# Two-layer attention and mixture-of-experts kernel: the loads of both accumulators wait for both last scatters

## The reference

```
x = x + cross_attention(norm(x), keys and values = ctx and the tokens themselves)   # layer 0
x = x + experts(norm(x), 8 experts, each token goes to 2, inner width 256)          # layer 0
x = x + cross_attention(norm(x), keys = values = ctx, masked)                       # layer 1
x = x + experts(norm(x), 32 experts, each token goes to 8, inner width 192)         # layer 1
experts(t) = sum over the chosen e of weight(t, e) * (silu(t @ gate_e) * (t @ up_e)) @ down_e
```

## Time and profile before

| | us |
|---|---|
| median of three runs | 943.73 |
| lowest and highest of them | 940.0 and 945.9 |
| the profiled execution, its time | 939.34 |
| its span, from the first to the last instruction | 937.6 |

### The profile page before, as it was taken

The page is one execution under the profiler, slowest core; times in us unless marked ns, Lnnn a source line. Parts: engine busy times, 40 slices in busy tenths (PEclk is TensorE's granted clock), DMA queues, the critical chain, the costliest instruction groups (busy, mean ns, idle before and its releaser), DMA issues.

```text
span 937.6 us, 19263 instructions
## 1 busy us (share of the span) xinstructions
PE 796.3 (85%) x5266; PEld 437.7 (47%) x5267; DVE 559.9 (60%) x1596; ACT 516.6 (55%) x780; POOL 433.0 (46%) x355
## 2 busy tenths in 40 slices
PE   4999999999848999966888735999889899999995
PEld 2444455555425544433443414555555455555552
DVE  5553445555564555685676625576557575667475
ACT  6533234455445776333544523786777787778760
POOL 3882000200014676130075662467776666667862
PEclk9999999999968999998899876999999999999998
DMA  8562200201116696790120102898899897998777
GB/s 287 180 217 98 77 34 23 46 24 35 34 26 207 181 253 147 213 315 7 53 69 26 48 24 67 219 261 251 202 253 262 234 303 192 250 223 260 143 112 276
DMA packets 85842, 143.74 MB, mean 153 GB/s; under 512 B 19462, under 2 KB 36102, under 8 KB 85793
## 3 DMA queue, kind: packets, MB, share of 16 engines
q1 hardware_dynamic: 58880, 93.49, 30.5%
q0 software_dynamic: 24320, 49.45, 24.4%
q10 hardware_dynamic: 2592, 0.19, 0.2%
HBM read 106.25 MB, written 41.28 MB: 157 GB/s over the span
## 4 chain that ended last, share of the span: by engine, by line
PE 49%; issue 13%; DMA 12%; DVE 11%; ACT 6%; DVEq 2%; ACTq 2%; another core or an unknown queue 2%; POOL 1%; SPq 1%; POOLq 0%
PE pst L194 38%; PE pst L1368 4%; DMA mid<-moe_normalised_rows,row_no 3%; DMA x_rows<-mid,row_no 2%; PE pst L515 2%; DMA big<-in_L_ffn_wo_dram 2%; DMA xT<-moe_normalised_rows,row_no 2%; PE pst L1341 2%; DVE big L1247 1%; ACT mid L1431 1%; DMA x_rows<-xT,row_no 1%; PE pst L1423 1%; DVE mid L1520 1%; ACT big L1240 1%
## 5 line engine op out<-in xcount | busy, mean ns | idle before, releaser
L194 PE MATMUL pst<-big,mid 128*128 (+1 forms) x1392 | 272.1, 346 | 19.4 <-ACT mid L1431 13.1
L1056 POOL DMA_INDIRECT moe_tokens_of_experts<-token_no,small x70 | 73.3, 1047 | 271.3 <-DVE small L1141 253.7
L194 PEld LDWEIGHTS pst<-big,mid 128*128 128x128 f16 x1392 | 132.9, 98 | 122.1 <-issue 29.0
L1368 PE MATMUL pst<-big,mid 128*128 x520 | 128.9, 380 | 0.1
L1431 ACT ACTIVATE mid<-pst 128x1024 f16<-128x1024 f16 x100 | 102.5, 1025 | 29.7 <-PE pst L1341 19.9
L1622 POOL DMA_INDIRECT x_rows<-mid,row_no x48 | 90.9, 1894 | 48.8 <-DMA x_rows<-xT,row_no 22.5
L1622 POOL DMA_INDIRECT x_rows<-xT,row_no x46 | 87.7, 1906 | 52.3 <-DMA x_rows<-mid,row_no 20.9
L1520 DVE SCALAR_TENSOR_TENSOR mid<-pst,small,mid 128x192 f32<-128x192 f32 (+1 forms) x100 | 42.7, 427 | 106.6 <-ACT mid L1437 87.2
L194 PE MATMUL pst<-ctxN,mid 128*128 128x512 f16 x384 | 92.5, 399 | 3.1 <-ACT mid L647 3.1
L1245 DVE TENSOR_TENSOR big<-big (+2 forms) x40 | 74.6, 1864 | 3.7 <-issue 0.2
L1612 POOL DMA_INDIRECT mid<-moe_normalised_rows,row_no x52 | 54.9, 1055 | 46.1 <-DVE row_no L1503 22.1
(11 more groups left out here) (234 smaller groups left out, 1273.8 us busy)
## 6 DMA issues: line engine op xcount, KB each, us to landing
big<-in_L_ffn_w_gate_dram SPq DMA_DIRECT2D x32, 768.0 KB
big<-in_L_ffn_wi_dram SPq DMA_DIRECT2D x8, 1024.0 KB
big<-in_L_ffn_w_down_dram SPq DMA_DIRECT2D x32, 256.0 KB
big<-in_L_ffn_w_down_dram SPq DMA_DIRECT2D x64, 128.0 KB
moe_normalised_rows<-xn SPq DMA_DIRECT2D x18, 256.0 KB, 2.0
mid<-in_ctx_dram SPq DMA_DIRECT2D x16, 256.0 KB, 4.9
big<-in_ctx_turned_dram SPq DMA_DIRECT2D x16, 256.0 KB, 5.2
x_rows<-big SPq DMA_DIRECT2D x16, 256.0 KB, 3.8
```

The lines of the kernel that those rows point to most:

```text
L194: last = nc.tensor.matmul(dst, stationary(a, c), moving(b, c), start=(k == 0), stop=(k == 3 * len(parts) - 1))
L1056: nc.gpsimd.indirect_dma_start(out=self.tab_d[:, :], out_offset=bass.IndirectOffsetOnAxis(ap=self.addr[j % 2][:, k:k + 1], axis=0), in_=to ...
L1368: last = nc.tensor.matmul(bank(6 + p), hT[:, k, :], self.d[:, s, h, c, :], start=(q == 0), stop=(q == len(seq) - 1))
```

## The change

`sums_back` had two waits: one of `done_s` at its first count ahead of the eight loads of `acc_d[1]`, and one at its second count ahead of the eight loads of `acc_d[0]`. Now there is one wait, for the second count, ahead of all sixteen. The order of the loads, their semaphores and all else stay. It is called once after each expert stage.

```diff
         def sums_back(sp, stage):
-            sp.wait_ge(done_s, 2 * stage + 1)
+            sp.wait_ge(done_s, 2 * stage + 2)
             for i in range(NT):
                 sp.dma_start(x_sb[:, i, :], acc_d[1][i * P:(i + 1) * P, :]).then_inc(first_in, 16)
-            sp.wait_ge(done_s, 2 * stage + 2)
             for i in range(NT):
                 sp.dma_start(part[:, i, :], acc_d[0][i * P:(i + 1) * P, :]).then_inc(x_in_s[i], 16)
```

## The result

Twenty runs of each kernel: before 939.64 us (937.33 to 949.14), after 949.46 us (940.48 to 955.24). The ratio of the fast executions (all but the one of 955.24 us) is recorded as 1.0066, with a 95% interval of 1.0039 to 1.0093: the change makes the kernel slower by 6.2 us (3.7 to 8.7). The medians are 9.8 us apart and the plain means of all twenty (941.1 and 949.0) 7.9 us. Two more comparisons, made later with the experiments, gave 1.0107 (1.0077 to 1.0138) and 1.0068 (1.0036 to 1.01); the mean of the three is +0.8%, some 7.5 us.

A forecast was written before the change was run, and what follows sets the result against it. Matmuls bound the whole run; DMA alone the first hand-over, with loads, TensorE and GpSimd's sums nearly level at the second. +1.6 and +1.9 make +3.5 us, on the median 943.73 giving 947.2 us; range 941 to 952.

The forecast's parts named there:

- The scatter alone, 4.8 us: Both hand-overs: the last even scatter, with no loads beside it, takes 4.8 us, against 8.6 and 6.1 before.
- The rival that the loads were not what slowed it: Both hand-overs: the even scatter stays slow without loads beside it; together +8.4, 952.1 us; chance 10%.
- Eight loads alone, 8.1 us: Both hand-overs: eight accumulator loads with no scatter beside them take 8.1 us, against 11.3 and 9.4 before.
- First `add_rest` 13 us after S: First hand-over: VectorE's first `add_rest` starts 13 us after the start of the last even scatter, not 11.4.
- TensorE's wait, 2.3 us: First hand-over: TensorE's wait for the normalised rows grows from 0.70 to 2.3 us.
- The clock, put down as a rival with 15%: After the first hand-over's wait: TensorE's clock drops, scores at half pace, +1.7, so +5.2 and 948.9 us; chance 15%.
- First hand-over: predicted +1.6: First hand-over: the first eight loads have landed at 394.8 against 393.23, +1.6 us.
- Second hand-over, +1.9 us: Second hand-over: later loads delay `add_rest` and the sums; VectorE's sums end at 934.1 against 932.2, +1.9 us.
- The weight loads behind, at nothing, and issued as before: Behind the first hand-over's loads: weight loads issued as before, covered by 25 us of attention 1, cost nothing; +1 us uncovered.
- The gain from nothing beside the scatter: Both hand-overs: scatter and loads alone are so much shorter that the kernel gains; total -2, 941.7 us; chance 15%.
- The sign that attention 1 and experts 1 keep their length to 3 us: Stages between the hand-overs: the prediction is wrong if either changes its length by more than 3 us.

The follow-up runs named there:

- e1: Kernel before, with only the first hand-over's loads waiting for both scatters; 918.05 us against 917.53, ratio 1.0029 (0.9997 to 1.006).
- e5: Changed kernel with a semaphore for each odd-accumulator load and loads ordered in pairs, odd 0, 1, even 0, 1 and so on; ratio 1.0012 to the kernel before.
- e10: The changed kernel once more, unaltered, measured against the kernel before; ratio 1.0068 (1.0036 to 1.01).
- e3: Changed kernel with 12 more matmuls in TensorE's wait at the first hand-over; 921.3 us, ratio 1.005 (1.0019 to 1.0081) to the kernel before.

## Why the prediction was right, and where it was not

The direction and the range held: 949.46 us lies in 941 to 952, and slower by 0.66% is "within 1%" (by the medians it is 1.05%). The mechanism held too: the loads start later by what the scatter takes alone, and more is lost than the shorter transfers give back. The forecast of +3.5 us was too low; the interval of the result (3.7 to 8.7 us) begins above it. That 947.2 us came so near to 949.46 is partly luck: it started from a median of three executions, 943.73 us, where twenty gave 939.64, 4.1 us less, and this made up for much of what the sum lacked. By its steps:

- **The scatter alone, 4.8 us:** 5.0 and 5.0 us in the changed kernel, 4.8 to 5.1 in all late versions. The rival that the loads were not what slowed it is out: with the loads gone from its side it was never above 5.1 us.
- **Eight loads alone, 8.1 us:** 8.9 and 8.7 us. The start of the run was the nearest row and still 0.6 to 0.8 us too short. By the Trainium skill (DMA: Bandwidth & Descriptors, Anatomy of one DMA) the estimate was 6.8 us. The page gives that fit for one DMA issued by GpSimd, and here are eight in a row on SyncE's queue; the traces are 2 us above it.
- **First `add_rest` 13 us after S:** 13.96.
- **TensorE's wait, 2.3 us:** 3.31, and 3.20 and 4.02 in the other two profiles of the changed kernel. The missing microsecond is that of the loads.
- **The clock, put down as a rival with 15%:** this is the term that the sum lacked. It fell in all four profiles in which TensorE waited 2.7 us or more there (scores 9.79, 10.50, 10.53 and 10.89 us) and in none of the others (7.94 in each). The argument against it was that waits of 0.70 and 1.14 us had not done it; the sum itself made a wait of 2.3 us followed by that of 1.14, and the trace had no row for such a pair. A wait of 2.72 us was enough (e1); no run has one of 2.3 us, so whether the predicted wait would have done it is open. The Trainium skill's rule (TensorE: Matmul & The Clock Gate, Part 1) is that the clock is lowered when TensorE is idle and comes back only when it is kept busy. The trace agrees here (0.50 near the end of the 3.31 us wait, 1.00 again only at 411.2, 3.7 us into the scores), and the rule deserved more than 15%. First hand-over: predicted +1.6, with the clock +3.3, measured +4.7.
- **Second hand-over, +1.9 us:** +2.9. GpSimd's sums began 17.2 us after S and VectorE's ended at 24.2, predicted 16.5 and 23: again the 0.7 us of the loads, and the rest in sums that run wholly beside each other. Alone one of VectorE's takes 0.68 us, beside GpSimd's up to 1.79, and the four took 5.62 instead of 4.66 us. The Trainium skill has this as a lock (SBUF — State Buffer, SBUF: two separate sides): a VectorE operation with two operands in SBUF and a GpSimd operation that reads SBUF exclude each other. The trace agrees: the last `add_rest`, with one operand in PSUM, kept their 0.61 us pace when GpSimd had begun (939.01).
- **The weight loads behind, at nothing, and issued as before:** their first issue went from 394.65 to 400.13, 1.7 us later from S. No run shows a price for it, and e5, where the loads are as late, has none that can be told.
- **The gain from nothing beside the scatter:** both transfers did get shorter, by 3.6 and 2.4 us, but it decided from the point where the two together are under 11.3 us, and they took 14.0. It is out.
- **The sign that attention 1 and experts 1 keep their length to 3 us:** by the one pair of profiles this sign spoke against the prediction, experts 1 being 4.0 us longer. The experiments take the weight out of it: the same instructions took 330.0 to 339.6 us, and in e10, the changed kernel again, 335.5, as in the kernel before (335.6). It was a poor sign.

With the measured loads and sums in their places, and the clock in the sum, it is 2.6 + 2.1 + 2.9 = +7.6 us, about the mean of the three comparisons (7.5, which range from 6.2 to 9.8).

## What to carry to other kernels

Two transfers that slow each other can still be worth overlapping: compare the end of the pair (11.4 against 14.0 us), not the length of each. Before a wait on the critical path is moved, ask what the engine behind it does to its clock; a few cheap matmuls in the gap (e3), or loads in the order of use with a wait for each in place of a wait for all eight (e5), took back what the later start had cost there. And where one stage wanders by 10 us from run to run, read a change of 3 us from marks inside the trace, with the time as the second witness.

## What the hardware showed that was not expected

- A 128-row accumulating scatter took 4.8 to 5.1 us alone. At the first hand-over, with loads issued at the same instant, it took 8.0 us beside four loads of 256 KB and 7.8 to 8.6 beside eight, and 6.7 us beside eight that read another tensor (one execution). At the second, where the loads came 1.0 to 1.8 us later, it took 5.2 to 6.1 us. Four loads or eight made no difference; that the head start does is not shown by itself.
- The granted clock was still 1.00 after an idle wait of 2.72 us and 1.1 us of transposes, fell to 0.50 some 0.4 us into the next wait (e1), and came back only after some 6 us of scores. Yet the wait of 3.58 us behind those scores left it at 1.00 (e1 and e10), where in the kernel before the clock fell after it.
